# Triangular solve of a delta rule by blocks of 32 rows, in place and in 32-column tiles

## What is computed

```python
kb = k * beta[..., None]; v = v * beta[..., None]      # q and k are normalised
A = where(strict_lo, kb @ k.T, 0.0)
Tinv = solve_triangular(eye + A, eye, lower=True, unit_diagonal=True)
u, w = Tinv @ v, Tinv @ kb
def step(S, xs):                                       # chunk after chunk
    attn = where(strict_up, 0.0, q_i @ k_i.T)
    u_i = u_i - w_i @ S
    o_i = q_i @ S + attn @ u_i
    return S + k_i.T @ u_i, o_i
```

## Time and profile before

| | |
|---|---|
| time, median of 3 runs | 1272.36 us (1266.75 to 1273.87) |
| span of the profiled execution | 1263.7 us |
| time of the profiled execution around its span | not in the profile |
| TensorE busy | 1102.6 us, 87% |
| VectorE busy | 867.7 us, 69% |
| GpSimd busy | 559.6 us, 44% |
| ScalarE busy | 515.0 us, 41% |
| the costliest group of TensorE, the solve products (L674) | 93.1 us |

### The profile page before, as it was taken

The page is one execution under the profiler, slowest core; times in us unless marked ns, Lnnn a source line. Parts: engine busy times, 40 slices in busy tenths (PEclk is TensorE's granted clock), DMA queues, the critical chain, the costliest instruction groups (busy, mean ns, idle before and its releaser), DMA issues.

```text
span 1263.7 us, 22566 instructions
## 1 busy us (share of the span) xinstructions
PE 1102.6 (87%) x7730; PEld 841.4 (67%) x7730; DVE 867.7 (69%) x2268; ACT 515.0 (41%) x936; POOL 559.6 (44%) x995
## 2 busy tenths in 40 slices
PE   4988889698799899899899899989989989987892
PEld 2645558577567777677586686777767666856782
DVE  4888986854666866866876776676686674556477
ACT  4767754415123512521521442351351244744561
POOL 4233435256037526544734843762652224344452
PEclk9989999888899999999999999999999999989996
DMA  6543441431001501330250160130110263223488
GB/s 169 168 145 131 129 154 57 179 98 66 19 1 43 180 35 37 112 105 1 76 182 1 59 193 1 43 127 13 34 60 35 85 217 97 89 76 110 132 268 310
DMA packets 86783, 127.47 MB, mean 101 GB/s; under 512 B 28304, under 2 KB 62608, under 8 KB 84496
## 3 DMA queue, kind: packets, MB, share of 16 engines
q1 hardware_dynamic: 79472, 106.30, 26.3%
q0 software_dynamic: 7200, 19.74, 4.3%
HBM read 66.47 MB, written 59.55 MB: 100 GB/s over the span
## 4 chain that ended last, share of the span: by engine, by line
PE 50%; DVE 11%; POOL 6%; issue 5%; ACT 4%; another core or an unknown queue 1%; DMA 1%; SPq 1%; ACTq 0%; DVEq 0%; POOLq 0%
PE bank L674 7%; PE bank L579 5%; PE bank L559 4%; PE bank L727 3%; PE bank L506 2%; PE bank L886 2%; ACT arena L1053 2%; PE bank L737 2%; PE bank L546 2%; PE bank L777 2%; PE bank L569 2%; PE bank L645 2%; POOL orn L1420 2%; PE bank L654 2%; POOL arena L1405 2%
## 5 line engine op out<-in xcount | busy, mean ns | idle before, releaser
L958 ACT ACTIVATE arena<-bank 128x512 f32<-128x512 f32 (+1 forms) x326 | 171.3, 545 | 457.7 <-PE bank L569 142.7
L1533 DVE SCALAR_TENSOR_TENSOR arena<-arena,param 128x512 f32<-128x512 f32 x144 | 106.2, 751 | 23.5 <-ACT arena L981 20.0
L1467 POOL DMA_INDIRECT results<-arena x78 | 76.5, 981 | 100.9 <-DVE arena L2089 72.6
L1403 POOL TENSOR_TENSOR arena<-arena 128x126 f32<-128x126 f32 (+22 forms) x217 | 90.2, 415 | 37.3 <-DVE arena L1633 21.8
L1387 POOL COPY arena<-arena 32x128 f32<-32x128 f32 x128 | 51.6, 403 | 103.0 <-DVE arena L1623 97.1
L674 PEld LDWEIGHTS bank<-arena 128*128 128x128 f32 x768 | 92.2, 198 | 7.1 <-issue 6.9
L1405 POOL TENSOR_TENSOR arena<-arena 128x126 f32<-128x126 f32 (+22 forms) x217 | 86.9, 400 | 17.0
L674 PE MATMUL bank<-arena 128*128 128x128 f32 x768 | 93.1, 282 | 0.0
L886 PE MATMUL bank<-arena 128*128 128x128 f32 x624 | 87.4, 286 | 1.1 <-ACT arena L1216 0.7
L1339 POOL DMA_INDIRECT slots_x<-arena x64 | 63.5, 992 | 49.2 <-DVE arena L1828 31.9
L886 PEld LDWEIGHTS bank<-arena 128*128 128x128 f32 x624 | 80.3, 201 | 2.5 <-issue 2.4
(11 more groups left out here) (269 smaller groups left out, 2682.0 us busy)
## 6 DMA issues: line engine op xcount, KB each, us to landing
arena<-slots_x SPq DMA_DIRECT2D x78, 129.0 KB
slots_x<-rows_of_no_token SPq DMA_DIRECT2D x8, 1161.0 KB
xt<-x_in SPq DMA_DIRECT2D x16, 512.0 KB, 4.7
kq_T<-kq SPq DMA_DIRECT2D x8, 1024.0 KB, 3.8
kq<-kq_T SPq DMA_DIRECT2D x8, 1024.0 KB
arena<-results SPq DMA_DIRECT2D x32, 256.0 KB
arena<-ffn_in SPq DMA_DIRECT2D x7, 768.0 KB, 4.1
vT<-v_T SPq DMA_DIRECT2D x8, 514.0 KB
```

The costliest lines, as they stand in the source:

```text
L958: free(act.activation(out_, in_, func, **kw), name)
L1403: own.link(pool.tensor_tensor(tmp, rows32[:, m0:, k].unsqueeze(2).broadcast_to([P, nm, k]), units[:, 0:k, k].unsqueeze(1).broadcast_to([P, ...
L1467: pool.indirect_dma_start(results[:, :], bass.IndirectOffsetOnAxis(ap=dest[:, n % YS:n % YS + 1], axis=0), ys[:, n % YS, :], None).then_in ...
L1533: ins = V.scalar_tensor_tensor(cv[:, k % 4, :], pre[:, j, d:d + GT], param[:, at + d:at + d + 1], cv[:, k % 4, :], ALU.mult, ALU.add)
```

## The change

A step q of the solve now computes only the 32 rows of block q: the weights are 32 columns of NT, and the product goes to the 32 partitions of PSUM that belong to block q. The four chunks are staggered: diagonal s takes block s+1-t of every chunk t for which there is one, so six diagonals have 1, 2, 3, 3, 2 and 1 blocks, and the products of a head for the blocks of one diagonal are issued one after the other. VectorE subtracts 32 partitions at a time, in place in UW; ScalarE copies the product of the diagonal inverse into UW instead of Y, so that Y is read only by `front_product`. The orders of the work around it are rewritten on TensorE, ScalarE and VectorE.

```diff
+DIAGONALS = tuple(tuple((t, s + 1 - t) for t in range(T) if 1 <= s + 1 - t < NQ) for s in range(T + NQ - 2))
...
@@ TensorE, body @@
-                def solve(q):
-                    for t in range(T):
-                        n = f"solve{t}{q}.{i}"
-                        o = open_bank(pe, n, t)
-                        for h in range(t * H, t * H + H):
-                            oo = o[:, (h % H) * P:(h % H + 1) * P]
-                            last = mm(oo, NT[:, h, :], (Y if q == 1 else UW)[:, h, :], start=True, stop=True)
-                        full(last, n)
-
-                if x:
-                    context()
-                    rows()
-                else:
-                    keys_loaded(1)
-                    front_gram(1, 0)
-                    front_gram(1, 1)
-                solve(1)
-                if x:
-                    queries()
-                else:
-                    front_gram(1, 2)
-                    front_gram(1, 3)
-                solve(2)
-                if x:
-                    masked_scores(0)
-                solve(3)
-                if x:
-                    turned_scores(0)
-                    masked_scores(1)
-
-                for t in range(T):
-                    if ahead:
-                        front_values(i + 1, t)
+                def solve(s):
+                    mine = DIAGONALS[s]
+                    for t, q in mine:
+                        open_bank(pe, f"solve{t}{q}.{i}", t)
+                    for h in range(H):
+                        for t, q in mine:
+                            qq = slice(QB * q, QB * q + QB)
+                            last = mm(banks[t][qq, h * P:(h + 1) * P], NT[:, t * H + h, qq], UW[:, t * H + h, :],
+                                      start=True, stop=True)
+                            if h == H - 1:
+                                full(last, f"solve{t}{q}.{i}")
+
+                def effects(t):
                     drained(pe, f"solve{t}{NQ - 1}.{i}")
...
+                if x:
+                    context()
+                    rows()
+                    solve(0)
+                    if ahead:
+                        front_values(i + 1, 0)
+                    solve(1)
+                    queries(0)
+                    solve(2)
+                    queries(1)
+                    solve(3)
+                    if ahead:
+                        front_values(i + 1, 1)
+                    masked_scores(0)
+                    solve(4)
+                    effects(0)
+                    solve(5)
+                    effects(1)
+                    turned_scores(0)
+                    masked_scores(1)
+                    if ahead:
+                        front_values(i + 1, 2)
+                    effects(2)
+                    values(0)
+                    turned_scores(1)
+                    if ahead:
+                        front_values(i + 1, 3)
+                    effects(3)
+                    values(1)
+                    masked_scores(2)
+                    if ahead:
+                        front_gram(i + 1, 0)
+                else:
+                    keys_loaded(1)
+                    for t in range(T):
+                        front_gram(1, t)
+                        solve(t)
+                    front_values(1, 0)
+                    solve(4)
+                    front_values(1, 1)
+                    effects(0)
+                    solve(5)
+                    front_values(1, 2)
+                    effects(1)
+                    front_values(1, 3)
+                    effects(2)
+                    effects(3)
...
@@ ScalarE @@
-                    evac(Y[:, t * H:(t + 1) * H, :], heads(o), n)
+                    evac(UW[:, t * H:(t + 1) * H, :], heads(o), n)
...
                     front_squares(i, range(T))
+                    if i == 0:
+                        act.wait_ge(sem("long_ready"), CK * NG)
                     front_product(i)
                 if x:
                     rows()
-                    probs(0)
-                if i == 0:
-                    act.wait_ge(sem("long_ready"), CK * NG)
                 for t in range(T):
                     if ahead:
                         front_values(i + 1, t)
-                    if x and t == 1:
-                        probs(1)
+                    if x and 1 <= t < 3:
+                        probs(t - 1)
...
@@ GpSimd, front_rows @@
-                        drained(pool, f"solve{t}{NQ - 1}.{i - 1}")
+                        drained(pool, f"solve{t}0.{i - 1}")
...
@@ VectorE, body @@
-                def solve(q):
-                    for t in range(T):
+                def solve(s):
+                    for t, q in DIAGONALS[s]:
                         n = f"solve{t}{q}.{i}"
                         o = filled(dve, n)
-                        drained(dve, f"solve{t}0.{i}")
-                        tt = slice(t * H, (t + 1) * H)
-                        free(V.tensor_tensor(UW[:, tt, :], Y[:, tt, :], o[:, :].rearrange("p (h c) -> p h c", h=H),
-                                             ALU.subtract), n)
...
+                        if q == 1:
+                            drained(dve, f"solve{t}0.{i}")
+                        rr, tt = slice(QB * q, QB * q + QB), slice(t * H, (t + 1) * H)
+                        free(V.tensor_tensor(UW[rr, tt, :], UW[rr, tt, :],
+                                             o[rr, :].rearrange("p (h c) -> p h c", h=H), ALU.subtract), n)
...
+                if x:
+                    solve(0)
+                    solve(1)
+                    queries(0)
+                    solve(2)
+                    queries(1)
+                    solve(3)
+                    scores(0)
+                    solve(4)
+                    effects(0)
+                    solve(5)
+                    effects(1)
+                    scores(1)
+                    effects(2)
+                    values(0)
+                    effects(3)
+                else:
+                    filled(dve, f"N{T - 1}.{i}")
+                    for t in range(T):
+                        front_gram(1, t)
+                        solve(t)
+                    front_units(1)
+                    solve(4)
+                    effects(0)
+                    solve(5)
+                    for t in range(1, T):
+                        effects(t)
```

More of the change, by code:

```diff
@@ L537, in rows, with queries @@
                     transpose_rows(xn_x, [f"x1T0.{i}", f"x1T1.{i}"], (next(cross_bank), next(cross_bank)))
-                def queries():
+                def queries(*ms):
                     drained(pe, f"x1T0.{i}")
                     drained(pe, f"x1T1.{i}")
-                    for m in range(CK):
+                    for m in ms:
                         n = f"qx{m}.{i}"
@@ L920, in _ @@
             steps(1)
-            queries()
+            queries(0, 1)
             steps(1)
@@ L1900, in body, with effects @@
                     anykey()
-                def solve(q):
-                    for t in range(T):
+                def solve(s):
+                    for t, q in DIAGONALS[s]:
                         n = f"solve{t}{q}.{i}"
                         o = filled(dve, n)
-                        drained(dve, f"solve{t}0.{i}")
-                        tt = slice(t * H, (t + 1) * H)
-                        free(V.tensor_tensor(UW[:, tt, :], Y[:, tt, :], o[:, :].rearrange("p (h c) -> p h c", h=H),
-                                             ALU.subtract), n)
-                if not x:
-                    filled(dve, f"N{T - 1}.{i}")
-                    front_gram(1, 0)
-                    front_gram(1, 1)
-                solve(1)
-                if x:
-                    queries()
-                else:
-                    front_gram(1, 2)
-                    front_gram(1, 3)
-                solve(2)
-                if x:
-                    scores(0)
-                else:
-                    front_units(1)
-                solve(3)
-                if x:
-                    scores(1)
-                for t in range(T):
+                        if q == 1:
[3 more added lines that the diff above has]
+                                             o[rr, :].rearrange("p (h c) -> p h c", h=H), ALU.subtract), n)
+                def effects(t):
                     n = f"wa{t}.{i}"
@@ L1940, in body @@
                     free(last, n)
-                    if x and t == 2:
-                        values(0)
+                if x:
[25 more added lines that the diff above has]
+                        effects(t)
                 if x:
```

8 lines of the change are left out of this document (removed).

## The result

The changed kernel takes 1301.56 us (median of 4 runs, 1299.65 to 1304.24), the kernel before 1271.09 beside it: ratio 1.0258, 95% interval 1.0228 to 1.0287. It is 30.5 us slower. I forecast 1282, 9.9 slower: the side was right, the size a third of what came, and the time lies 2.6 us above my range.

The account below looks back on a forecast made before the run. A body lasts as TensorE takes to its last gram, plus a fixed tail. Body 0 -4.5, bodies 1 and 6 -3.0 each, 7 -2.4, 2 to 5 +16.0 and +6.8: +9.9 on 1272.4, so 1282 us, range 1256 to 1299.

Parts of the forecast that it names:

- body 0: First body, bound by VectorE: the units come at about 264.6, so -4.5 us; bounds 0 and -6.
- bodies 2 to 5: Bodies with slot blocks ahead of the loads: 16.0 us lost net of gains, plus 6.8 us for clock restarts.
- Products: Solve products on TensorE: six diagonals of 1.12 us, 6.7 us a body instead of 10.7, so 4.0 removed.
- The rival without overlap: Column tiles on TensorE don't run beside each other: 5.3 us more products a body, 1315 us; chance 0.07.
- the one with two at a time: Only two column tiles run together, and switches are dear: +0.9 and +0.7 in eight bodies, 1295 us; chance 0.08.
- Waits between diagonals: TensorE waiting for VectorE's subtractions: 2.4 us a body against 1.3 in the old order, net gain 3.0 a body.
- The walk: TensorE's body 2 in the old order, stepped through with timeline durations: ends at 477.7 against 477.55 traced, with 1.3 us of waits.
- Loads: Moved transposes on TensorE wait for kq and v in bodies 2 to 5: 9.0, 6.4, 8.1, 5.8 us, 29.3 in all.
- The rival of loads in time (1247): Both loads have landed when the first diagonal ends, so no wait is left: -25 us, 1247 us; chance 0.17.
- that of shorter stalls: Load waits in bodies 2 to 5 average 5 us instead of 7.3 and the clock holds: 1266 us; chance 0.08.
- Clock: TensorE restarts at half clock after each of four load waits: 1.7 us each, +6.8 us; upper bound 3 each.
- Nothing waits: -3.0 each: Bodies 1 and 6, with no slot blocks in flight: no wait for loads, so each gains the full 3.0 us.

Follow-up runs that it names:

- fills_scatter_late: The changed kernel with SyncE's slot-block fills behind the loads and GpSimd's scatter behind front_rows: 1259.67 us, ratio 0.994; run again 1236.73 us, 0.9923.
- tiles_alone: The kernel before, its own order of work and no staggering, with the 32-column products in place: 1274.0 us, ratio 1.0062.
- fills_late: The changed kernel with only SyncE's two slot-block fills moved behind the loads of the next group: 1278.43 us, ratio 1.0098.
- scatter_late: The changed kernel with only GpSimd's scatter moved behind front_rows (in body 7 behind the last diagonal): 1294.88 us, ratio 1.0181.
- fv_back: The changed kernel with TensorE's transposes of chunks 0 and 1 moved back behind diagonals 4 and 5: 1282.92 us, ratio 1.0133.
- after_again: The changed kernel run once more, unaltered, where the kernel before took 1247.16 us: 1273.0 us, ratio 1.022.
- fills_late_again: The kernel of fills_late run once more, unaltered, where the kernel before took 1247.16 us: 1236.56 us, ratio 0.9923.

## Why the prediction was right in its sign and wrong in its size

| part | forecast | measured |
|---|---|---|
| body 0 | -4.5 | -3.3 |
| body 1 | -3.0 | -2.0 |
| bodies 2 to 5 | +22.8 | +32.6 |
| body 6 | -3.0 | +2.8 |
| body 7 and what follows | -2.4 | +4.1 |
| sum | +9.9 | +34.2 |

The measured parts are differences between the starts of L645/L646 in the two timelines.

*Products: right.* A three-block diagonal takes 1.00 us to the next instruction (447.62 to 448.62), where I had 1.12 with the ways in and out. In a body without stall or late signal (31.7 in fills_scatter_late, 2.55 of it idle, against 33.87 with 0.55 idle) the work went down by 4.1 us; the forecast was 4.0 (the diagonals alone are 0.7 shorter than forecast, the rest around them longer by as much). tiles_alone shows that this is the overlap of the column tiles. The rival without overlap is out, and so is the one with two at a time.
The Trainium skill ("TensorE: Matmul & The Clock Gate", Measured speedup vs the span model) would give three column tiles 2.38 of 3 (measured there with 512 moving columns, here they are 128); here 24 instructions take what 8 take, 1.00 us, the full 3.

*Waits between diagonals: the new ones right, the old ones too large.* The forecast had 2.4 us; clean bodies show 2.3 to 2.9, the largest ahead of diagonal 5 with 1.78 (I said 1.3), as scores(0) stands ahead of diagonal 4's subtractions. But I set 1.3 us of waits in the old order against them, and the trace of before has 0.55. So the net gain of a clean body is 1.8 to 2.1 us, not 3.0; about 5 us over bodies 2 to 5, and 1 in each other one. A walk whose end agrees with the trace can still have its waits wrong; they are to be read from the timeline. The walk also ended at 477.55 as the last gram's end, which is the third's; the fourth ends at 480.61. That changed no number, for the order behind 477.55 is the same in both kernels.

*Loads: right in cause and nearly in size.* 32.4 us instead of 29.3, in the order forecast (10.1, 6.6, 9.8, 6.0 for 9.0, 6.4, 8.1, 5.8), none in bodies 1 and 6. The transposes start about 1 us behind the last traffic (441.63; 53 GB/s in 440:442) rather than with it. In body 2 I had read the landing as 445.9; the way I used for the other bodies gives 445.2 (217 of 375 GB/s in 444:446), so 0.7 of the 9.0 us was a misreading. fills_late shows that the slot blocks ahead of the loads make the stall. The rival of loads in time (1247) falls, and so does that of shorter stalls.

*Clock: right, a little small.* I took 1.7 us for each restart, where my own rows give 5.67 - 3.84 = 1.8. Bodies 2 to 5 without their stall are 34.0, 33.6, 34.2 and 33.9, against 31.7 (even) and 32.1 (odd) for the undisturbed bodies 3 to 6 of fills_scatter_late: 8.1 us for four restarts instead of 6.8. That the clock is all of these 8.1 us isn't shown, as no run took its part out by itself.

*The step that failed: "Nothing waits: -3.0 each", for body 6, and -2.4 for body 7.* Of the 24.3 us between the forecast and the measured sum these two bodies make 12.3 (about 1 us in each is the smaller gain above, and 1.5 stand behind body 7). Of the rest, 5.3 are the smaller gain of bodies 2 to 5, 4.4 their stalls and restarts, and 2.2 are in bodies 0 and 1. Nothing waited for loads, but VectorE waited for TensorE's signals beside the scatter. scatter_late takes body 6 from 36.6 to 31.7, and so does the set without late signals; there body 7 falls from 33.6 to 30.0. I had walked the diagonals with 0.26 to 0.3 us of latency from TensorE to VectorE for all bodies, and the trace of before shows otherwise. Its VectorE, in the second solve step of body 2, starts 2.8 us after TensorE's step (442.75), and in the first 1.1 us (436.84 after 435.74) with the same work:

```profile
445.56 2.48 DVE L1908 TENSOR_TENSOR arena<-arena,bank 128x512 f32<-128x512 f32 x4 [1.85 <-remote]
```

There it cost nothing: TensorE is idle for 0.55 us of this stretch with the scatter (body 2) and without it (body 1). A step of four banks and its filler leave some 5 us until the next step needs the result. The staggered diagonals leave about 3, and then the lateness comes through. fv_back and fills_late show it in bodies 2 to 5 too (36 to 38 us), where the change itself had it hidden in its stalls. With no late signals the change still loses 2.2% (after_again, stalls of 32.0 us in all); without the stalls too it gains 0.8% (fills_late_again).

*Body 0.* The units came 5.0 us earlier (264.26; 4.5 was the forecast), and so did VectorE's L1676, which takes GpSimd's inverses (294.37 for L1656's 299.41). 1.7 us of it was lost between there and TensorE's products: ScalarE's L1074 stands behind its L1170, an exponential for a gate, and that one came only 3.3 us earlier (299.03 for L1150's 302.35). *Behind body 7* the change is 1.5 us longer; this was not followed.

## What to carry to other kernels

A wait for a load that is moved forward blocks everything behind it on that engine: find what is queued ahead of the load in its own queue, and move that first. When an order is tightened, look in the old trace for signals that arrive late but are hidden, for the new order has less slack for them. Try two repairs together as well as apart, as one delay can cover another (20 and 10 us alone, 40 together).

## What the hardware showed that was not expected

- TensorE's signals reached VectorE up to 4 us late beside GpSimd's indirect stores, in the sets where the kernel before takes 1268 to 1271 us, and not at all in those where it takes 1247 to 1249. The same program (fills_late) has ratios of 1.0098 and 0.9923 there. What the two kinds differ in is open, and so is whether it belongs to the chip.
- The kinds differ most at the end of the kernel, in the experts, where GpSimd issues 78 more indirect stores: from body 7's start the change takes 328 us in the one and 306 in the other. The late signals are there too. Of VectorE's idle time before L2106, which reads the experts' products, 21.2 us end with "remote" in the one (first line, the changed kernel) and none in the other (second line, after_again). How much of the 22 us they make wasn't tested.

```profile
L2106 DVE TENSOR_TENSOR arena<-bank,arena 128x128 f32<-128x128 f32 x78 | 22.4, 288 | 70.1 <-remote 21.2
L2106 DVE TENSOR_TENSOR arena<-bank,arena 128x128 f32<-128x128 f32 x78 | 22.4, 288 | 54.7 <-PE bank L907 28.5
```

- VectorE takes 686 ns for a subtraction on 32 partitions and 683 ns for the same on 128, per instruction in the costliest groups.
- Three tiles of 128 rows and 32 columns run wholly beside each other (24 instructions in 1.00 us), and a tile of 32 columns alone takes as long as one of 128 (0.113 us).
